# Eight-by-eight window attention: keys moved by SBUF transfers instead of TensorE, values' product in the rotation's bank, projection one iteration back

## The reference, cut to what matters

```
qkv  = xw @ qkv_w.T + qkv_b                 # xw: 256 windows x 64 positions x 64 channels
q, k = rope2(q), rope2(k)                   # each channel pair turned by row or column position
attn = softmax(q * 8 ** -0.5 @ k.T)         # per window and head, 64 x 64
out  = (attn @ v) @ proj_w.T + proj_b
```

## Time and profile before

| | |
|---|---|
| median of three runs | 1708.08 us |
| the profiled execution, its own time | 1710.65 us |
| its span, first to last instruction | 1708.8 us |
| mean granted TensorE clock | 0.967 |
| first stage (window attention) | about 2 to 340 us of the span |

### The profile page before, as it was taken

How to read it: one execution, slowest core, us unless ns; L and a number is a source line. 1 busy time by engine, 2 the same in 40 slices (tenths; PEclk the granted TensorE clock), 3 DMA queues, 4 the chain that set the end, 5 groups by cost and what they waited for, 6 DMA issues and landing times.

```text
span 1708.8 us, 83280 instructions
## 1 busy us (share of the span) xinstructions
PE 1568.4 (92%) x29546; PEld 1169.1 (68%) x29546; DVE 1212.2 (71%) x3605; ACT 1041.2 (61%) x2053; POOL 613.4 (36%) x923
## 2 busy tenths in 40 slices
PE   5899999779999999999986899999999999999996
PEld 3677777657777777777764667667667667667663
DVE  1566666547888878788755778778778778778762
ACT  2565655444444444444421578878878878878876
POOL 3242222166666666666622212212212212212210
PEclk9999999869999999999995899999999999999997
DMA  3201001034444444444420233333333333333332
GB/s 105 79 25 31 25 30 31 12 103 117 126 123 121 121 120 127 124 122 122 123 74 22 66 84 83 88 83 83 88 83 83 88 83 83 88 83 83 88 77 56
DMA packets 134833, 143.15 MB, mean 84 GB/s; under 512 B 42770, under 2 KB 90258, under 8 KB 134514
## 3 DMA queue, kind: packets, MB, share of 16 engines
q1 hardware_dynamic: 126450, 116.07, 26.0%
q10 hardware_dynamic: 8320, 26.22, 5.7%
HBM read 66.42 MB, written 16.99 MB: 49 GB/s over the span
## 4 chain that ended last, share of the span: by engine, by line
PE 66%; issue 8%; DVE 8%; DMA 5%; ACT 4%; SPq 4%; POOL 2%; ACTq 1%; DVEq 1%; POOLq 0%
PE ps_D L901 12%; DVE prob L1469 4%; PE ps_D L811 4%; PE ps_D L687 4%; DMA k_d<-kpad 3%; PE ps_AV L918 3%; PE ps_OT L830 3%; SPq L465 2%; PE ps_J L1009 2%; PE ps_J L977 2%; PE ps_AV L838 2%; PE ps_J L959 2%; PE ps_OT L653 2%; PE ps_J L1040 2%; PE ps_AV L697 2%
## 5 line engine op out<-in xcount | busy, mean ns | idle before, releaser
L1211 ACT ACTIVATE prob<-ps_D 128x1024 bf16<-128x1024 f32 x448 | 459.4, 1029 | 121.2 <-PE ps_D L901 119.3
L1181 ACT ACTIVATE prob<-ps_D 100x512 f32<-100x512 f32 x256 | 139.0, 595 | 166.2 <-PE ps_D L811 166.2
L811 PE MATMUL ps_D<-tile_a,key_patch 64*100 64x128 f32 x2048 | 175.9, 289 | 0.0
L560 POOL TENSOR_TENSOR tile_a<-q_st,q_mask 128x512 f32<-128x512 f32 x128 | 135.2, 1056 | 112.5 <-PE ps_D L811 93.5
L901 PE MATMUL ps_D<-tile_a,w_parts 128*128 128x256 bf16 x1024 | 153.9, 276 | 11.0 <-DVE xg L1506 3.0
L901 PE MATMUL ps_D<-tile_b,w_parts 128*128 128x256 bf16 x1024 | 152.5, 274 | 12.4 <-DVE xg L1506 3.4
L807 PE MATMUL ps_D<-mT,key_rows 64*100 64x128 bf16 x1024 | 124.4, 226 | 25.1 <-ACT prob L1181 25.1
L534 POOL TENSOR_TENSOR rstd_bin<-veps_bin,minus_half 128x2 f32<-128x2 f32 x64 | 44.2, 691 | 269.4 <-DVE veps_bin L1272 269.4
L1373 DVE TENSOR_REDUCE m_sb<-ps_D 128x4 f32<-128x400 f32 x256 | 134.5, 566 | 8.9 <-PE ps_D L788 8.5
L811 PEld LDWEIGHTS ps_D<-tile_a,key_patch 64*100 64x100 f32 x2048 | 140.3, 167 | 0.0
L534 POOL TENSOR_TENSOR rstd_ret<-veps_ret,minus_half 128x2 f32<-128x2 f32 x64 | 46.6, 728 | 247.7 <-DVE veps_ret L1272 247.7
(11 more groups left out here) (179 smaller groups left out, 4010.6 us busy)
## 6 DMA issues: line engine op xcount, KB each, us to landing
tile_a<-xg SPq DMA_DIRECT2D x384, 64.0 KB, 2.0
tile_b<-xg SPq DMA_DIRECT2D x384, 64.0 KB, 2.0
key_st<-k_d SPq DMA_DIRECT2D x128, 162.0 KB, 3.0
tile_b<-v_d ACTq DMA_DIRECT2D x128, 120.0 KB
tile_b<-v_d ACTq DMA_DIRECT2D x64, 160.0 KB
w_exp<-experts SPq DMA_DIRECT2D x64, 129.0 KB, 2.3
xT<-in_x SPq DMA_DIRECT2D x32, 256.0 KB, 2.6
k_d<-kpad SPq DMA_DIRECT2D x64, 64.0 KB, 2.9
```

Source lines behind the costliest of these rows:

```text
L560: gp.tensor_tensor(q_block[:, par, :].rearrange("c (p h q) -> c p h q", h=NH, q=NQ)[:, own, :, :], q_st[:, par, :].rearrange("c (p a q) -> ...
L811: mm = pe.matmul(s_loc[x][0:NKL, u * P:(u + 1) * P], key_patch[rows_of(x), par, at * NKL:(at + 1) * NKL], q_block[rows_of(x), par, at * P: ...
L1181: act.activation(prob1[0:NKL, 2 * g + x, :], s_loc[x][0:NKL, :], ACT.Exp).then_inc(T2["exp_done"], 1)
L1211: act.activation(sgn[:, k % 4, :], unit(k, par)[:, :], ACT.Sign).then_inc(BN["sign"], 1)
```

## The change: what it does

- The key products and their four masked copies on ScalarE are gone, with their two constant tables. In their place SyncE issues eight SBUF-to-SBUF transfers an iteration (`keys_spread`), one for each row group and head: 8 rows of 512 positions of `rot`, written as 8 rows of eight runs of 64 columns (256 bytes each) into `k_tok`. They wait for the rotation; four signal the first group of maxima and four the second. Before the loop GpSimd clears `tile_a` as a second fill, and the engines wait for eight fills instead of seven.
- `tok_v` writes the lower half of bank T, after VectorE has read the rotation product of i + 2 from it. `tok_qk` waits for the values' copies of the iteration before the one it follows.
- The order on TensorE becomes: top(i), qk(i+2), scores(i), v(i+1), max(i+1) group 0, project(i-1), max(i+1) group 1, values(i). ScalarE: top(i), sin(i+2), exponentials(i), values' copies(i+1). VectorE: normalize(i-1), rope(i+2), maxima(i+1), rows(i-1).
- SyncE's queue: input 0, 10 loads, input 1, keys 0 (waiting for the first rotation), 12 later loads, input 2, keys 1, 12 later loads, input 3, keys 2, the last 9 later loads with the expert table, and then in the loop an input and one iteration's keys in turn.

The lines that only drop the two constant tables, their tiles and the semaphore names are left out:

```diff
@@ -356,7 +352,7 @@
         def _(sp):
             loads = [(ident[:, :], a["ident"]), (cos[:, :], a["cos"]), (sin[:, :], a["sin"]), (w_qk[:, :], a["w_qk"]),
                      (b_qk[:, :], a["b_qk"]), (w_v1[:, :], a["w_v1"]), (w_p1[:, :], a["w_p1"]), (w_p1_rows[:, :, :], a["w_p1_rows"]),
-                     (b_v1[:, :], a["b_v1"]), (top_rows[:, :, :], a["top_rows"]), (key_shift[:, :], a["key_shift"]), (head_row[:, :], a["head_row"])]
+                     (b_v1[:, :], a["b_v1"]), (top_rows[:, :, :], a["top_rows"])]
             later = [(q_mask[:, :], a["q_mask"]), (ones_h[:, :, :], a["ones_h"]), (q_rows[:, :], a["q_rows"]), (m_sb[:, :], a["m_init"]),
                      (decay[:, :], a["decay"]), (decay_q[:, :], a["decay_q"]), (key_rows[:, 0, :], a["key_rows"]),
                      (key_rows[:, 1, :], a["key_rows"]), (decay_k[:, :], a["decay_k"]), (w_kq2[:, :], a["w_kq2"]), (w_v2[:, :], a["w_v2"]),
@@ -372,18 +368,34 @@
                 sp.wait_ge(T1["v_ps"], times(i - 1))
                 sp.dma_start(xT[:, par, :], a["x"][bass.ds(i, 1), :, :].rearrange("a r n -> (a r) n")).then_inc(T1["x_in%d" % par], 16)
 
+            def keys_spread(i, par):
+                sp.wait_ge(T1["rope"], times(i + 1))
+                settle(sp)
+                for j in range(4):
+                    for e in range(2):
+                        r = 32 * j + HD * e
+                        sp.dma_start(k_tok[par][r:r + HD, :, NKT * e:NKT * (e + 1)],
+                                     rot[r + 2 * HD:r + 3 * HD, par, :].rearrange("r (w k) -> r w k", w=WIN)).then_inc(T1["k_in%d%d" % (par, j // 2)], 16)
+
             for signal in T1.values():
                 sp.sem_inc(signal, 1)
             x_in(0, 0)
             for dst, src in loads:
                 sp.dma_start(dst, src).then_inc(s_w, 16)
+            x_in(1, 1)
+            sp.wait_ge(s_const, NFIRST_CONST)
+            keys_spread(0, 0)
             for n, (dst, src) in enumerate(later):
                 sp.dma_start(dst, src).then_inc(s_later, 16)
-                if n % 8 == 7 and n < 24:
-                    x_in(n // 8 + 1, (n // 8 + 1) % 2)
+                if n in (11, 23):
+                    x_in(n // 12 + 2, n // 12 % 2)
+                    keys_spread(n // 12 + 1, (n // 12 + 1) % 2)
             with sp.Fori(2, NT // 2) as j:
                 x_in(j * 2, 0)
+                keys_spread(j * 2 - 1, 1)
                 x_in(j * 2 + 1, 1)
+                keys_spread(j * 2, 0)
+            keys_spread(NT - 1, 1)
 
             sp.wait_ge(s_const, NCONST)
             for at in (0, FLAT - EDGES):
@@ -481,7 +493,7 @@
 
         @block.gpsimd
         def _(gp):
-            fills = [(tile_b[:, :, :], 0.0), (top1[:, :, :], 0.0), (ones_32[:, :, :], 0.0),
+            fills = [(tile_b[:, :, :], 0.0), (tile_a[:, :, :], 0.0), (top1[:, :, :], 0.0), (ones_32[:, :, :], 0.0),
                      (ones_32[0:C, 0, 0:HD], 1.0), (ones_32[0:C, 1, HD:2 * HD], 1.0), (ones_32[C:P, 0, 2 * HD:3 * HD], 1.0),
                      (ones_32[C:P, 1, 3 * HD:4 * HD], 1.0), (experts[:, :, NEXP:NEXP + 1, :], 0.0), (xnp[:, :, :], 0.0), (xn_fg[:, :, :], 0.0),
                      (xn_r[:, :, :], 0.0), (xn_r[:, :, C:C + 1], 1.0), (kd3[:, :, :], 0.0), (minus_half[:, :], -0.5), (zeros[:, :], 0.0),
@@ -630,32 +642,26 @@
                 pe.wait_ge(T1["x_in%d" % par], times((pair + 1) * 16))
                 pe.wait_ge(T1["cos_mul"], times(i))
                 pe.wait_ge(T1["sin_in"], times(i))
-                pe.wait_ge(T1["k_sb"], times(i * 4))
+                pe.wait_ge(T1["v_sb"], times((i - 1) * 4))
                 settle(pe)
                 pe.matmul(bank["T"][:, :], w_qk[0:C, :], xT[0:C, par, :], start=True, stop=True)
                 pe.matmul(bank["J1"][:, :], w_qk[C:P, :], xT[C:P, par, :], start=True, stop=True).then_inc(T1["qk_ps"], 1)
 
-            def tok_keys(i, par):
-                pe.wait_ge(T1["rope"], times(i + 1))
-                settle(pe)
-                for half, name in enumerate(("T", "J1")):
-                    at = slice(256 * half, 256 * (half + 1))
-                    pe.matmul(bank[name][:, at], key_shift[:, :], rot[:, par, at], start=True, stop=True).then_inc(T1["k_ps"], 1)
-
             def tok_v(i, par):
                 pe.wait_ge(T1["v_sb"], times(i * 4))
-                pe.wait_ge(T1["h_done"], times(i - 2))
+                pe.wait_ge(T1["cos_mul"], times(i + 2, NT))
                 settle(pe)
                 for p in range(4):
                     for ab in range(2):
                         for e in range(2):
-                            at = 256 + (p * 2 + ab) * 32
-                            mm = pe.matmul(bank["OT"][rows_of(e), at:at + 32], xT[rows_of(e), par, window(ab, p)], w_v1[rows_of(e), 32 * e:32 * (e + 1)],
+                            at = (p * 2 + ab) * 32
+                            mm = pe.matmul(bank["T"][rows_of(e), at:at + 32], xT[rows_of(e), par, window(ab, p)], w_v1[rows_of(e), 32 * e:32 * (e + 1)],
                                            start=True, stop=True)
                 mm.then_inc(T1["v_ps"], 1)
 
-            def tok_max(i, par, g):
-                pe.wait_ge(T1["k_sb"], times((i + 1) * 4))
+            def tok_max(i, pair, par, g):
+                pe.wait_ge(T1["rope"], times(i + 1))
+                pe.wait_ge(T1["k_in%d%d" % (par, g)], times((pair + 1) * 64))
                 pe.wait_ge(T1["exp_done"], times((i - 1) * 4 + 2 * g + 2))
                 settle(pe)
                 for p in range(4):
@@ -706,7 +712,6 @@
 
             def tok_project(i):
                 pe.wait_ge(T1["attn_out"], times(i + 1))
-                pe.wait_ge(T1["v_sb"], times((min(i + 3, NT) if isinstance(i, int) else i + 3) * 4))
                 pe.wait_ge(T1["h_done"], times(i))
                 settle(pe)
                 for y in range(4):
@@ -722,27 +727,24 @@
                 last = isinstance(i, int)
                 more = not last or i + 1 < NT
                 tok_top(i)
-                if not last or i > 1:
-                    tok_project(i - 2)
-                if more:
-                    tok_keys(i + 1, 1 - par)
-                tok_scores(i, par)
                 if not last or i + 2 < NT:
                     tok_qk(i + 2, j + 1, par)
+                tok_scores(i, par)
                 if more:
-                    tok_max(i + 1, 1 - par, 0)
                     tok_v(i + 1, 1 - par)
-                    tok_max(i + 1, 1 - par, 1)
+                    tok_max(i + 1, *after(j, par), 0)
+                if not last or i:
+                    tok_project(i - 1)
+                if more:
+                    tok_max(i + 1, *after(j, par), 1)
                 tok_values(i, par)
 
             tok_qk(0, 0, 0)
-            tok_keys(0, 0)
+            tok_qk(1, 0, 1)
             tok_v(0, 0)
-            tok_max(0, 0, 0)
-            tok_max(0, 0, 1)
-            tok_qk(1, 0, 1)
+            tok_max(0, 0, 0, 0)
+            tok_max(0, 0, 0, 1)
             pairs(pe, tok)
-            tok_project(NT - 2)
             tok_project(NT - 1)
             pe.wait_ge(s_later, 16 * NLATER)
             pe.wait_ge(s_const, NCONST)
@@ -1075,22 +1077,13 @@
                     for e in range(2):
                         at = HD * (2 * e + ab)
                         act.activation(v_tok[par][rows_of(e), :, ab, :, at:at + HD],
-                                       bank["OT"][rows_of(e), 256:512].rearrange("k (p s h d) -> k p s h d", p=4, s=2, d=HD)[:, :, ab, :, :], ACT.Copy).then_inc(T1["v_sb"], 1)
+                                       bank["T"][rows_of(e), 0:256].rearrange("k (p s h d) -> k p s h d", p=4, s=2, d=HD)[:, :, ab, :, :], ACT.Copy).then_inc(T1["v_sb"], 1)
 
             def tok_sin(i):
                 act.wait_ge(T1["qk_ps"], times(i + 1))
                 act.wait_ge(T1["rope"], times(i))
                 settle(act)
                 act.activation(t_sin[:, :], bank["J1"][:, :], ACT.Identity, bias=b_qk[:, 1:2]).then_inc(T1["sin_in"], 1)
-
-            def tok_keys(i, par):
-                act.wait_ge(T1["scores"], times(i - 1))
-                for half, name in enumerate(("T", "J1")):
-                    act.wait_ge(T1["k_ps"], times(i * 2 + half + 1))
-                    for e in range(2):
-                        act.activation(k_tok[par][:, 4 * half:4 * (half + 1), NKT * e:NKT * (e + 1)],
-                                       bank[name][:, 256 * half:256 * (half + 1)].rearrange("r (w k) -> r w k", w=4),
-                                       ACT.Identity, scale=head_row[:, e:e + 1]).then_inc(T1["k_sb"], 1)
 
             def tok(j, par):
                 i = j * 2 + par
@@ -1098,21 +1091,18 @@
                 act.wait_ge(T1["top_ps"], times(i + 1))
                 act.activation(top1_T[:, :], s_tok[3][:, 0:P], ACT.Copy, scale=-1.0).then_inc(T1["top_sb"], 1)
                 more = not last or i + 1 < NT
-                if more:
-                    tok_keys(i + 1, 1 - par)
```

(24 more changed lines are left out.)

## The result

The changed kernel takes 1698.51 us (median of five, 1695.64 to 1702.66), the kernel before 1708.08: ratio 0.9939, 95% interval [0.9921, 0.9956], 9.6 us less. A second measurement on another chip gave 0.9924 [0.9894, 0.9954]. The forecast of 1686 had the direction and, to a tenth of a microsecond, the new period; the first three iterations took 9.8 us more than before.

What follows compares the result with a forecast made beforehand. TensorE's chain of waits was taken as the bound: 30 iterations x 0.95 = 28.5 us, less 7 at the start, plus 1 at the end, gives 22.5 off 1708.1, say 1686 us; range 1674 to 1702.

Steps and rivals of the forecast that it cites:

- the new period: One loop iteration: 8.35 us instead of 9.30, a gain of 0.95 us, bounds 0.7 to 1.00.
- The piece by piece sum: TensorE's path through one iteration, from top to values, added from the old profile's pieces: 8.11 us instead of 9.11.
- the loop's turn: End of each iteration: 0.19 us beyond the chain's pieces, put down to the turn of the loop.
- the term: TensorE's path in each iteration: the key products leave it, minus 1.06 us.
- rival 1: Loop: VectorE becomes the bound, 8.75 us with five wake-ups of 0.25, time 1698; chance 0.14.
- rival 2: Loop: the input lands late for qk; at the largest landing, 4.7 us, period 9.26 and time 1713; chance 0.08.
- The key transfers: SyncE's queue: eight issues at 0.66 us, 5.3 us an iteration, landing 1.9 us before group 1 wants them; nothing on the path.
- rival 3: SyncE's queue sets the period, slower: 1786 at 1.3 us an issue; chance 0.08 together with maxima waiting for the last landing.
- my own test: Key-transfer runs: above 56 ns each by the 512-byte minimum, not above by the section sparing copies inside SBUF.
- The fill and the first keys: Before the loop: GpSimd's fill of tile_a and the first key transfers cost plus 3.5 us, bounds 1.5 to 6.
- The start: First iterations: 3.5 us for fill and first keys, 3.5 for input 4 behind the later expert table; together plus 7.
- The end: After iteration 30: v fills the wait; if the clock holds, values and maxima run up to 2 us faster, taken as 1.

Runs made afterwards that it cites:

- The products put back: Two unused 128 x 256 fp32 products of the keys' size behind each transpose, against the changed kernel with the expert table's load early: 1708.08 us (one execution).
- seventeen products in the wait: Changed kernel with seventeen unused 128 x 256 fp32 products behind the values of iteration 1, where TensorE waits for input 4: 1697.85 us (one execution).
- the kernel with the loads early: Changed kernel with the expert table and 19 small loads issued before the first keys, input 2 ahead of the remaining thirteen: 1681.88 us, again 1686.01.

## Why the prediction was right in the loop and wrong in the sum

- *The new period*, 8.35 us: measured 8.42 over the 26 steps on which the old 9.30 rests, a gain of 0.88 a step for the 0.95 reckoned and inside its bounds; over 27 steps it is 0.95, but only because the kernel before has one step of 11.51 us. The piece by piece sum holds: 8.10 us on the chain for 8.11, with qk 1.06 for 1.12 and the wait 1.31 with v inside (207.13 to 208.44). What lies above it is the stall at the loop's turn, some 0.3 a step where I had 0.19. The products put back confirm that the term is on the path, at 0.75 to 0.98.
- *VectorE* (rival 1) is close and does not bind: the reductions take 2.48 us and end at 211.40, 0.35 before the values; no wait for them stands in the loop. That the measured 1698.5 is the price of this rival, and lies inside the range that was stretched over it, is coincidence.
- *The late input* (rival 2) is in no step of the loop, where TensorE never waits for a transfer from 100 to 300 us. It came true in iterations 0 and 2 alone, by the queue's order and not by a slow landing in the steady state.
- *The key transfers*: 0.73 us an issue for my 0.66; no wait for a landing, and rival 3 needed twice as many. The queue's packets from 100 to 300 us, changed kernel and kernel before (packets, MB, share of 16 engines):

```profile
q1 hardware_dynamic: 17209, 9.34, 23.8%
...
q1 hardware_dynamic: 3168, 5.77, 10.1%
```

  Before, where nearly all of it is input from HBM in packets of 2 KB, a packet takes 0.101 x 200 x 16 / 3168 = 102 ns. The changed kernel issues 23 inputs in that time, some 338 us of the engines' 762; the rest leaves some 30 ns for each of about 13900 short packets, an estimate, and less than the 56 I took. By my own test that speaks for the section "Why small descriptors are slow (HBM only)" of the Trainium skill (DMA: Bandwidth & Descriptors), which spares copies inside SBUF. But by the byte these runs cost 2.4 times what the inputs' packets do, so the trace does not show that they are spared altogether, and it says nothing of the 512-byte minimum of the same page's Specifications. On how many engines a transfer ran no row here tells.
- *The fill and the first keys*: 3.5 us; measured 3.7.
- *The start, wrong.* The step that failed is "The expert table ... now goes out behind two groups of key transfers, some 7 us later", with "I take 3.5" for the wait behind it. Three groups of key transfers stand ahead of the table, not two, 5.97 + 5.81 + 6.27 = 18.05 us of issues, and the queue stands for another 11.3 us at the first rotation with all loads behind it. The 7 has no working in the prediction, and two groups alone are 10.6 us at its own 0.66 an issue. The queue before stood too, 5.4 and 12.9 us, for an input's buffer to come free:

```profile
21.66 0.33 SPq L373 DMA_DIRECT2D xT<-in_x  x1
...
38.69 0.33 SPq L373 DMA_DIRECT2D xT<-in_x  x1
```

  The 29.4 us less these 18.3 are 11.1 of the 11.7 us by which the table goes out later. Input 4 right behind it cost 7.1 us of waiting, twice my 3.5, and the 4.5 us of slow clock after it (63.93 to 76.61, 12.7 us, against 8.2 from qk to transpose in the loop) had no term. Nor had the wait for input 2, 5.0 us, which went out at 30.78 instead of 21.66. The three steps took 9.8 us more than before where I had 0.65 more (3.5 less three times 0.95): the miss is 9.2 us. Of it 6.7 lie in iteration 2 and 2.5 in iterations 0 and 1; the wait for input 2 costs so little against the kernel before because that one stood there for 2.8 us at its rotation and then ran the key products. My bounds for the start, up to 13 in all, were passed as well (3.7 + 9.8 + 2.85 = 16.4).
- *The end*: 2 us were forecast, 0.95 for iteration 30 and 1; it was 4.5. The steps of iterations 30 and 31 keep the clock: 0.82 granted from 316 to 335 us before, 1.00 from 304 to 320 after.
- *The sum*: -22.5 forecast; in the profiles -16.6 for the stage and -15.0 in all. Of the further 5.4 us to the medians, both profiles lie off their medians in opposite directions. The later stages, whose code is the same, take 1365 to 1373 us from one execution to another in these runs; I have no cause for that, and it stays open.

So the gain in the loop was forecast rightly and the start was not: with the table in the queue's empty time the kernel gains 26.8 us, with the loads as well 24 to 30. That these lie near 22.5 is in part luck, for the end brought 2.5 us more than its term.

## What to carry to other kernels

When an issue that waits for computation is put into a queue that also holds loads, reckon the time at which the queue *reaches* each later entry, the waits included, and not the number of issues put ahead; whatever depends on no computation belongs in front of the first wait. A consumer moved earlier in its engine's order needs its input's issue time checked in the first iterations, not only in the steady ones. A wait's price on TensorE can be the wait and a slow clock after it: 7.1 + 4.5 us here.

## What the runs showed of the hardware

- An SBUF-to-SBUF issue of 16 KB in 64 runs of 256 bytes took SyncE 0.73 us in a row, against 0.66 for 64 KB in the rows of before; halves of it cost as much each, 11.7 us for 16, which made the period 12.6 us. An issue is paid by its number here.
- A 256 KB input behind the 2064 KB table in one queue landed after 7.9 us instead of 2.7.
- With seventeen products in the wait TensorE was idle for 1.7 us, worked for 7.5 and was idle for 1.9, and then went to 1.2 GHz for some ten microseconds. In the kernel with the loads early a pause of 1.92 us was followed by some ten microseconds at 1.2 GHz in one profile, and a pause of 1.94 by none in the other. In the kernel with qk behind the scores, which has gaps of 0.5 to 1.0 us, the granted clock was 0.91 to 0.97 in the loop.
- The stall at the loop's turn changed with code outside the loop: steps alternate between 8.32 and 8.56 us in the changed kernel and between 8.32 and 8.37 where twelve products stand in front of the loop, 2 to 3 us over the stage. The cause is not shown.
